# Moving the splits, the normalisation and the ranking of an attention and experts kernel into its batches of value matmuls

## The chip, the cores and the metric

One core of a Trainium2 chip (trn2) runs the whole program. The metric is the device time of one execution in microseconds (us). The median of 3 runs of the kernel before is 449.27 us (449.26 to 450.5).

## The reference

Four sequences of 256 tokens (D = 128) attend to a context of 1601 rows of 96 numbers, with 8 heads of 64, and then pass a mixture of 8 experts (2 chosen for each token) and one shared expert. Everything is float32.

```python
def xattn(x, context, Wq, Wk, Wv, Wo, bo):       # x is _layernorm(x)
    q = (x @ Wq).reshape(B, S, HEADS, DIM_HEAD).transpose(0, 2, 1, 3)
    k = (context @ Wk).reshape(B, L, HEADS, DIM_HEAD).transpose(0, 2, 1, 3)
    v = (context @ Wv).reshape(B, L, HEADS, DIM_HEAD).transpose(0, 2, 1, 3)
    attn = jax.nn.softmax(jnp.einsum('bhsd,bhld->bhsl', q, k) * scale, axis=-1)
    out = jnp.einsum('bhsl,bhld->bhsd', attn, v)
    return out.transpose(0, 2, 1, 3).reshape(B, S, INNER) @ Wo + bo
x = x + xattn(_layernorm(x), ctx_768, ...)
flat = _layernorm(x).reshape(T, d)
router_probs = softmax(flat @ router_w + router_b); topk_probs, topk_idx = top_k(router_probs, 2)
shared_out = gelu(flat @ sw1 + sb1) @ sw2 + sb2
h1 = gelu(einsum('td,edh->teh', flat, rw1) + rb1)
mixed = einsum('ted,te->td', einsum('teh,ehd->ted', h1, rw2) + rb2, weights)
x = x + shared_out + mixed
```

## The kernel before

The attention runs over 16 **pairs** of heads: 4 batches b times 4 pairs p, numbered 4b+p, so that pairs 0, 4, 8 and 12 open a batch. A pair has 13 chunks of 128 context rows (the last has 65), taken in 7 units of two chunks (the last unit has one). For each chunk TensorE (PE) computes the scores as three matmuls (lines 1165 to 1167), because each float32 operand is held as a high part in fp32r and a low part, the remainder; ScalarE (ACT) takes the exponential into `probs` (L766). When all scores of a pair are done, PE runs the pair's **batch of values**: 52 matmuls in the profile's count (L1181), probabilities times `v_sb`. After the batch come the **row sums** of the pair (L1046), a matmul with ones over the probabilities that were added up over the chunks. Adding them up is GpSimd's (POOL): one instruction for units 0 and 1 (L522) and one for each of units 2 to 5 (L524), each 128x1024; VectorE (DVE) then folds the two halves and adds unit 6 (L526, L527). PE's row sums wait for L527. In pair 0 POOL does L526 and L527 too, and in pairs 13 (units 4 and 5), 14 and 15 DVE does the adding.

Every engine goes through one list, `steps`, which `plan` writes: `main` is the order by hand (scores, quotients, and steps that follow an earlier pair by 2, 3 or 6 pairs, the table `behind`), and tasks for later pairs (maxima L1092 and L890, `g`) are put between by `plan`'s estimates. An engine takes from the list the steps that concern it, in order. These steps are touched by the change:

- **ctx**: the context of the next batch is split in 4 quarters, the high part by ACT (`high_part`, L705), the low part by POOL (`low_part`, L630). In batch b's pair p = 1 they stand one behind each of units 1 to 4, so between POOL's adds.
- **normalisation** of the tokens after attention: DVE takes moments in step `yt` (two pairs later, unit 3), POOL computes the inverse roots (L612 to L615, four small instructions) at the same step, and ACT writes the normalised tokens (`norm`, L711) behind unit 5, before the pair's last exponential.
- **rank** and **best**: the two largest router probabilities, on DVE (L938 to L952), then the weights on POOL (L669 to L674), behind unit 4 of pair 10.
- **w1**: the experts' first weights (128x2304) are split by POOL ahead of its loop (L651, L653). The raw weights lie at the start of `work`, whose first half is POOL's accumulators (two of 1024 columns, for pairs of even and odd number) and whose second half is `oT`, the attention's output (1024 columns for each of two batches), written by DVE in `quotient` (L837, L839).
- **stats**: the inverse roots of the first normalisation of batches 1 to 3, three times four small instructions on POOL in pair 0.

Of the kernel before, what the change touches and what calls it, by code (L numbers as in the profile page):

```python
# [52 lines left out]
def plan(batches, pairs, chunks, heads_per_pair, tiles, blocks, halves, experts):  # L53
# [3 lines left out]
    n_units = len(units)  # L57
    order = [(b, p) for b in range(batches) for p in range(pairs)]
    tasks = [("g", 0, 0)]
    n_v0 = 0  # L60
    for n, (b, p) in enumerate(order):
# [16 lines left out]
        if n == 0:  # L78
# [6 lines left out]
    behind = {(1, 2): [("ring", ("y",))], (3, 2): [("ring", ("yt",))], (5, 2): [("norm",)],  # L85
              (2, 3): [("ring", ("xt",))], (3, 3): [("ring", ("router",)), ("exp",)],
              (4, 3): [("rank",), ("best",)], (3, 6): [("ring", ("wrow",))]}
    main, held = [], []
    for n, (b, p) in enumerate(order):
        for u, unit in enumerate(units):  # L90
            for j, c in enumerate(unit):
                if p == 0 and b:
                    main.append(("ring", ("v", b, c)))
                main.append(("scores", (b, p, u, j)))
                if n and (u, j) in (((4, 0), (4, 1)) if n == 1 else ((0, 1), (1, 1))):
                    main.append(("quotient", order[n - 1] + ((u, j) in ((4, 1), (1, 1)),)))
            if (n, u) == (1, 3):
                main.append(("sums", order[0]))
            if p == 1 and b + 1 < batches and 0 < u <= blocks:
                main.append(("ctx", (b + 1, u - 1)))  # L100
            held += [("values", (b, p, u, j)) for j in range(len(unit))]
            if (b, p) == order[-2]:
                main += [("w2", e) for e in range(experts) if e * n_units // experts == u]
            for ago in (2, 3, 6):
                if n < ago:
                    continue
                qb, qp = order[n - ago]
                half = (qb + 1) * halves // batches - 1
                for x in behind.get((u, ago), []):
                    name = x[1][0] if x[0] == "ring" else x[0]  # L110
                    if qp == pairs - 1 and name in ("y", "yt", "xt"):
                        main.append(("ring", (name, qb)))
                    elif qp == pairs - 1 and name == "norm":
                        main.append((name, qb))
                    elif qp == pairs - 1 and (qb + 1) % (batches // halves) == 0:
                        main.append(("ring", (name, half)) if x[0] == "ring" else (name, half))
        main += held + [("sums", (b, p))] * (0 < n < len(order) - 1)
        held = []
# [6 lines left out]
    pe = dve = act = 0.0  # L125
# [30 lines left out]
    for i, x in enumerate(main):  # L156
        kind, w = x
# [47 lines left out]
def plan_experts(experts, chunks, halves, last_pair):  # L205
# [5 lines left out]
    b = last_pair[0]  # L211
# [6 lines left out]
    behind = {2: [("ring", ("yt", b))], 3: [("norm", b)]}  # L218
# [30 lines left out]
def build(nc, x, ctxT, WqkT, Wv, Wo, bo, router_w, router_b, sw1, sb1, sw2, sb2, rw1, rb1, rw2, rb2, out):  # L249
# [7 lines left out]
    T = S // P  # L257
# [15 lines left out]
    TH = HALF // P  # L273
    WLO = 32
# [29 lines left out]
    with ExitStack() as ctx:  # L304
# [3 lines left out]
        def sem(name):  # L308
            return ctx.enter_context(nc.semaphore(name))
# [47 lines left out]
        w1_sb = work[:].rearrange("p a b -> p (a b)")[:, 0:NE * H].rearrange("p (e h) -> p e h", e=NE)  # L357
# [79 lines left out]
        w_split = sem("w_split")  # L437
# [156 lines left out]
        def _(pool):  # L594
# [3 lines left out]
            def own(ins):  # L598
                done[0] += 1
                ins.then_inc(pool_done, 1)  # L600
# [48 lines left out]
            pool.wait_ge(s_w1, 32)  # L649
            pool.wait_ge(s_rw, 32)  # L650
            own(g.tensor_copy(w1_hi[:], w1_sb))  # L651
            then_own(g.tensor_copy(rw_hi[:], rw_sb[:]))
            g.tensor_tensor(w1_lo[:], w1_sb, w1_hi[:].bitcast(F32), ALU.subtract).then_inc(w_split, 1)  # L653
# [7 lines left out]
            pool.wait_ge(w_split, 3)  # L661
            pool.wait_ge(wrow_zero, 2)
            for kind, w in steps:
# [15 lines left out]
                if kind == "stats":  # L679
                    inverse_roots(slice(w * T, w * T + T), w + 1)  # L680
                if kind == "ring" and w[0] == "yt":
                    inverse_roots(slice(w[1] * T, w[1] * T + T), B + w[1] + 1)
# [14 lines left out]
        def _(act):  # L697
# [9 lines left out]
            def normal(src, tiles, round_no):  # L707

                act.wait_ge(rstd_ready, round_no)
                for t in tiles:  # L710
                    ins = nc.scalar.activation(xn[:, t, :], src[:, t, :], ACT.Identity, bias=shift[:, t:t + 1],  # L711
                                               scale=rstd[:, t:t + 1])
                ins.then_inc(xn_ready, 1)
# [11 lines left out]
            for kind, w in steps:  # L725
# [6 lines left out]
                elif kind == "normal":  # L732
                    normal(x_sb, range(w * T, w * T + T), w + 1)
                elif kind == "norm":
                    if w == 0:
                        act.wait_ge(*taken(("xn", 1)))
                    normal(x1, range(w * T, (w + 1) * T), B + w + 1)
# [70 lines left out]
        def _(dve):  # L808
# [189 lines left out]
        def _(pe):  # L998
# [51 lines left out]
            for kind, w in steps:  # L1050
                if kind == "sums":
                    row_sums(*w)
                if kind == "ring":
# [59 lines left out]
                    elif w[0] == "router":  # L1113
                        pe.wait_ge(w_split, 3)
# [83 lines left out]
                elif kind == "first":  # L1198

                    n, (h, e, k) = w, items[w]  # L1200
                    if n == 0:
                        pe.wait_ge(probs_ready, B * PAIRS * CH)
                        pe.wait_ge(w_split, 3)
# [60 lines left out]
```

## Time and profile before

| | |
|---|---|
| median of 3 runs | 449.27 us (449.26 to 450.5) |
| the profiled execution's own time | 449.95 us |
| its span, first to last instruction | 448.2 us |
| mean granted TensorE clock | 0.991 of full speed |
| PE busy | 432.9 us (97%) |
| DVE busy | 279.8 us (62%) |
| POOL busy | 257.9 us (58%) |
| ACT busy | 219.2 us (49%) |
| DMA packets | 7.30 MB, mean 16 GB/s |

The profile is of one execution. "Busy" is the time in which an engine has at least one instruction in work; a matmul's end is modelled, so a busy PE may be waiting for a fraction of a microsecond. The granted clock has two levels, 2.4 GHz (1.00) and 1.2 GHz (0.50). A bracket behind an instruction in the timeline tells how long its engine sat idle before it, and which instruction ended that.

### The profile page before, as it was taken

How to read it: one execution, taken by the hardware profiler on the slowest of the kernel's cores; microseconds unless marked ns; L12 is line 12 of the kernel's file. 1: busy time of each engine (PE TensorE's matmuls, PEld its weight loads, DVE VectorE, ACT ScalarE, POOL GpSimd, SP SyncE). 2: the span in 40 equal slices, each digit the busy share in tenths (PEclk: the TensorE clock that was granted, in tenths of full speed). 3: DMA queues.
4: the chain of work that ended last, by engine and by line, in shares of the span. 5: the costliest groups of instructions: out<-in, count | busy, mean ns of one | idle time of the engine just before them, and what ended most of it. 6: DMA issues, size and time to landing. Idle time of an engine off the chain costs nothing. (4 is left out here: it accounts for less than half of the span.)

```text
span 448.2 us, 7203 instructions
## 1 busy us (share of the span) xinstructions
PE 432.9 (97%) x2505; PEld 333.4 (74%) x2505; DVE 279.8 (62%) x555; ACT 219.2 (49%) x384; POOL 257.9 (58%) x183
## 2 busy tenths in 40 slices
PE   9999998999999979999999799999999999999996
PEld 7787767786877758777878586868776776777885
DVE  4785858695566648574458387844495775648443
ACT  3555524242752615335726152637334845686673
POOL 4979692746461938391719564635426620667771
PEclk9999999999999989999999999999999999999999
DMA  8300010000000020000000300000000000000000
GB/s 244 104 2 0 2 33 24 0 2 2 1 0 2 2 55 2 0 2 0 1 1 1 107 1 2 1 2 0 2 0 2 1 1 1 0 0 2 25 1 23
DMA packets 13834, 7.30 MB, mean 16 GB/s; under 512 B 9284, under 2 KB 12776, under 8 KB 13800
## 3 DMA queue, kind: packets, MB, share of 16 engines
q1 hardware_dynamic: 13800, 6.85, 6.2%
q8 instruction: 21, 0.34, 0.3%
q14 instruction: 13, 0.11, 0.1%
HBM read 6.29 MB, written 0.52 MB: 15 GB/s over the span
## 5 line engine op out<-in xcount | busy, mean ns | idle before, releaser
L766 ACT ACTIVATE probs<-ps 128x512 f32<-128x512 f32 (+1 forms) x208 | 123.8, 597 | 157.1 <-PE ps L1167 150.4
L890 DVE TENSOR_REDUCE maxes<-ps 128x1 f32<-128x402 f32 x256 | 131.7, 567 | 53.3 <-PE ps L1092 53.2
L524 POOL TENSOR_TENSOR work<-work,probs 128x1024 f32<-128x1024 f32 x54 | 128.8, 2385 | 14.3 <-ACT probs L766 12.3
L522 POOL TENSOR_TENSOR work<-probs 128x1024 f32<-128x1024 f32 x14 | 33.5, 2393 | 111.4 <-issue 107.7
L1181 PE MATMUL ps<-probs,v_sb 128*64 128x256 f32 (+1 forms) x832 | 93.4, 381 | 0.8 <-ACT probs L766 0.8
L1181 PEld LDWEIGHTS ps<-probs,v_sb 128*64 128x64 f32 (+1 forms) x832 | 59.1, 137 | 34.2 <-ACT probs L766 4.1
L1165 PE MATMUL ps<-g_hi,ctxT_hi 97*128 97x512 f32 (+1 forms) x208 | 84.4, 406 | 0.0
L1166 PE MATMUL ps<-g_lo,ctxT_hi 96*128 96x512 f32 (+1 forms) x208 | 82.8, 398 | 0.0
L1167 PE MATMUL ps<-g_hi,ctxT_lo 96*128 96x512 f32 (+1 forms) x208 | 82.3, 396 | 0.0
L1092 PE MATMUL ps<-ctxT_hi,g_hi 96*128 96x402 f32 x256 | 73.3, 363 | 0.4 <-DVE maxes L890 0.3
L690 POOL TENSOR_TENSOR g_lo<-probs,g_hi 128x512 fp32r<-128x512 f32 x32 | 40.6, 1292 | 35.5 <-ACT g_hi L788 34.3
L1092 PEld LDWEIGHTS ps<-ctxT_hi,g_hi 96*128 96x128 f32 x256 | 47.3, 191 | 14.8 <-issue 3.8
L1167 PEld LDWEIGHTS ps<-g_hi,ctxT_lo 96*128 96x128 f32 (+1 forms) x208 | 39.3, 189 | 10.2
L1165 PEld LDWEIGHTS ps<-g_hi,ctxT_hi 97*128 97x128 f32 (+1 forms) x208 | 38.9, 187 | 6.4 <-issue 0.8
L1166 PEld LDWEIGHTS ps<-g_lo,ctxT_hi 96*128 96x128 f32 (+1 forms) x208 | 39.3, 189 | 4.1
L526 DVE TENSOR_TENSOR work<-work 128x512 f32<-128x512 f32 x15 | 10.8, 719 | 38.3 <-POOL work L524 35.6
L837 DVE RECIPROCAL rden<-ps 128x128 f32<-128x128 f32 x32 | 30.3, 948 | 6.3 <-PE ps L1046 6.3
L744 ACT COPY v_sb<-ps 128x512 f32<-128x512 f32 (+1 forms) x39 | 22.9, 587 | 23.0 <-PE ps L1006 19.5
L976 DVE TENSOR_TENSOR probs<-ps,probs 128x512 f32<-128x512 f32 x32 | 20.6, 684 | 21.4 <-PE ps L1134 13.7
L803 ACT ACTIVATE probs<-ps,biasT 128x512 f32<-128x512 f32 x36 | 24.6, 688 | 17.7 <-PE ps L1006 16.0
L884 DVE CAST g_hi<-ps 96x512 fp32r<-96x512 f32 x16 | 10.9, 684 | 19.0 <-PE ps L1006 19.0
L1004 PE MATMUL ps<-wv_hi,ctxT_hi 96*128 96x512 f32 (+1 forms) x52 | 21.1, 406 | 0.1
(149 smaller groups left out, 536.1 us busy)
## 6 DMA issues: line engine op xcount, KB each, us to landing
raw<-in_ctx_T_dram SPq DMA_DIRECT2D x3, 600.4 KB, 4.4
work<-in_L_ffn_rw_dram SPq DMA_DIRECT2D x1, 1024.0 KB, 7.1
g_hi<-neg_row SPq DMA_DIRECT2D x60, 0.5 KB, 2.0
raw<-in_ctx_T_dram SPq DMA_DIRECT2D x3, 150.8 KB, 2.6
x_sb<-in_x_dram SPq DMA_DIRECT2D x1, 384.0 KB, 5.3
early<-in_WqkT_dram SPq DMA_DIRECT2D x1, 336.0 KB, 4.5
wo_sb<-in_L_xattn_Wo_dram SPq DMA_DIRECT2D x1, 256.0 KB, 5.1
out_dram<-x_sb SPq DMA_DIRECT2D x1, 256.0 KB, 2.2
```

The source lines that it names most:

```text
L522: ops.tensor_tensor(acc, probs[:, (n - 1) % SLOTS], pr, ALU.add).then_inc(summed, 1)
L524: ops.tensor_tensor(acc, acc, pr, ALU.add).then_inc(summed, 1)
L690: g.tensor_tensor(hid_lo[:, w % SPLITS, :], activations(w), hid_hi[:, w % SPLITS, :].bitcast(F32), ALU.subtract).then_inc(hid_lo_ready, 1)
L766: nc.scalar.activation(probs[0:rows, n % SLOTS, j, :], s_bank(chunk_no(*w))[0:rows, :], ACT.Exp, scale=SCALE).then_inc(probs_ready, 1)
L803: nc.scalar.activation(hid[:, n % 4, :], ps[:, n % HB, :], ACT.Gelu, bias=biasT[:, c:c + 1]).then_inc(hid_ready, 1)
L837: v.reciprocal(rden[:, q], sums_bank[:, q]).then_inc(rden_ready, 1)
L890: v.tensor_reduce(maxes[:, p % 2, i * T + t, blk:blk + 1], src[:, 0:BW], AX.X, ALU.max).then_inc(ring_taken, 1)
L1092: ins = mm(dst[:, 0:BW], g_hi[0:C, b % 2, 2 * p + i, t * P:(t + 1) * P], ctxT_hi[0:C, b % 2, k0:k0 + BW], start=True, stop=True)
L1165: mm(dst, ctxT_hi[:, b % 2, ks], gh, start=True, stop=False)
L1166: mm(dst, ctxT_hi[0:C, b % 2, ks], gl, start=False, stop=False)
L1167: ins = mm(dst, ctxT_lo[:, b % 2, ks], gh[0:C], start=False, stop=True)
L1181: ins = mm(o_bank[DH * i:DH * (i + 1), :], v_sb[0:rows, c, h * DH:(h + 1) * DH], probs[0:rows, n % SLOTS, j, i * S:(i + 1) * S], start=(c ...
```

## The change

It moves steps in the list, and splits w1 in two. In short:

- The four ctx steps of the next batch stand together at the end of a pair's scores, just before its batch of values: in pair 1 for batch 1, and in pairs 4 and 8 (the first pair of a batch instead of the second) for batches 2 and 3.
- The inverse roots are a step of their own (`roots`) and stand with `norm` at the same place, in pairs 5, 9 and 13.
- rank and best stand behind the batch of values of pair 10.
- w1 is split in two parts, experts 0 to 4 (128x1280) at the end of pair 0 and the rest (128x1024) at the end of pair 2. The raw weights are loaded to the last 2304 columns of `work`, over the last 256 columns of the odd accumulator and over both halves of `oT`; so DVE waits in the quotients of pairs 0 and 4 for the part that lies there.
- The three `stats` roots become one call over six columns (`stats` 3).

```diff
-    behind = {(1, 2): [("ring", ("y",))], (3, 2): [("ring", ("yt",))], (5, 2): [("norm",)],
+    behind = {(1, 2): [("ring", ("y",))], (3, 2): [("ring", ("yt",))], (n_units, 2): [("roots",), ("norm",)],
               (2, 3): [("ring", ("xt",))], (3, 3): [("ring", ("router",)), ("exp",)],
-              (4, 3): [("rank",), ("best",)], (3, 6): [("ring", ("wrow",))]}
+              (n_units + 1, 3): [("rank",), ("best",)], (3, 6): [("ring", ("wrow",))]}
...
-            if p == 1 and b + 1 < batches and 0 < u <= blocks:
-                main.append(("ctx", (b + 1, u - 1)))
             held += [("values", (b, p, u, j)) for j in range(len(unit))]
...
+            main += followers(n, u)
+        if p == (b == 0) and b + 1 < batches:
+            main += [("ctx", (b + 1, k)) for k in range(blocks)]
+        main += [("w1", k) for k in range(2) if n == 2 * k] + followers(n, n_units)
+        held += followers(n, n_units + 1)
         main += held + [("sums", (b, p))] * (0 < n < len(order) - 1)
...
+    W1_CUT = NE - PAIRS
...
-        w1_sb = work[:].rearrange("p a b -> p (a b)")[:, 0:NE * H].rearrange("p (e h) -> p e h", e=NE)
+        w1_sb = work[:].rearrange("p a b -> p (a b)")[:, 4 * PAIRS * S - NE * H:].rearrange("p (e h) -> p e h", e=NE)
...
-            pool.wait_ge(s_w1, 32)
             pool.wait_ge(s_rw, 32)
-            own(g.tensor_copy(w1_hi[:], w1_sb))
             then_own(g.tensor_copy(rw_hi[:], rw_sb[:]))
-            g.tensor_tensor(w1_lo[:], w1_sb, w1_hi[:].bitcast(F32), ALU.subtract).then_inc(w_split, 1)
...
+                if kind == "w1":
+                    es = (slice(0, W1_CUT), slice(W1_CUT, NE))[w]
+                    pool.wait_ge(s_w1, 32)
+                    then_own(g.tensor_copy(w1_hi[:, es], w1_sb[:, es]))
+                    g.tensor_tensor(w1_lo[:, es], w1_sb[:, es], w1_hi[:, es].bitcast(F32), ALU.subtract
+                                    ).then_inc(w1_split, 1)
+                    pool.wait_ge(w1_split, w + 1)
+                if kind == "stats" and w == B - 1:
+                    inverse_roots(slice(T, NT), B)
+                if kind == "roots":
+                    inverse_roots(slice(w * T, w * T + T), B + w + 1)
...
+                if p == 0 and b < 2:
+                    dve.wait_ge(w1_split, b + 1)
                 v.tensor_tensor(oT[:, b % 2, p, q], o_bank[:, q], rden[:, q], ALU.mult).then_inc(sums_taken, 1)
```

How the instructions stand, first **POOL from the end of pair 0 to pair 2**. Before (L522 opens a pair's adds, L630 is a ctx low part):

```order
L526 TENSOR_TENSOR work<-work 128x512
L527 TENSOR_TENSOR work<-work,probs 65x512
L522 TENSOR_TENSOR work<-probs 128x1024
L630 TENSOR_TENSOR ctxT_lo<-raw,ctxT_hi 96x402
L524 TENSOR_TENSOR work<-work,probs 128x1024
```

and with the change (the lines have moved on by 9: L531 is the old L522, L533 the old L524, L639 the old L630; L688 and L689 split w1, whose name stands here without its number):

```order
L535 TENSOR_TENSOR work<-work 128x512
L536 TENSOR_TENSOR work<-work,probs 65x512
L688 CAST w_hi<-work 128x1280
L689 TENSOR_TENSOR w_lo<-work,w_hi 128x1280
L531 TENSOR_TENSOR work<-probs 128x1024
L533 TENSOR_TENSOR work<-work,probs 128x1024 x4
L639 TENSOR_TENSOR ctxT_lo<-raw,ctxT_hi 96x402 x3
L639 TENSOR_TENSOR ctxT_lo<-raw,ctxT_hi 96x395
L531 TENSOR_TENSOR work<-probs 128x1024
L533 TENSOR_TENSOR work<-work,probs 128x1024 x4
L688 CAST w_hi<-work 128x1024
L689 TENSOR_TENSOR w_lo<-work,w_hi 128x1024
```

The low parts no longer stand between pair 1's adds but behind all five, and the two parts of w1 stand behind pair 0 and pair 2.

**POOL in pair 5**, before:

```order
L522 TENSOR_TENSOR work<-probs 128x1024
L630 TENSOR_TENSOR ctxT_lo<-raw,ctxT_hi 96x402
L524 TENSOR_TENSOR work<-work,probs 128x1024
L612 TENSOR_SCALAR veps<-mv 128x2
L613 TENSOR_TENSOR rstd<-veps,neg_half 128x2
L614 TENSOR_TENSOR shift<-mv,rstd 128x2
L615 TENSOR_SCALAR shift<-shift 128x2
L630 TENSOR_TENSOR ctxT_lo<-raw,ctxT_hi 96x395
```

and with the change:

```order
L531 TENSOR_TENSOR work<-probs 128x1024
L533 TENSOR_TENSOR work<-work,probs 128x1024 x4
L621 TENSOR_SCALAR veps<-mv 128x2
L622 TENSOR_TENSOR rstd<-veps,neg_half 128x2
L623 TENSOR_TENSOR shift<-mv,rstd 128x2
L624 TENSOR_SCALAR shift<-shift 128x2
```

Pair 5's four low parts have gone to the end of pair 4, and its roots stand behind the fifth add. Pair 9 reads the same. On PE nothing moves but three maxima of pair 10, which stand ahead of its batch of values instead of behind it.

## Rows read from the trace of the kernel before

**Rows 1.** Waits of PE: instruction waiting <- releaser: us in total, times, longest.

```profile
PE ps L1046 <- DVE work L527: 8.4, 5, 3.1
```

**Rows 2.** Timeline of PE: start, us, instruction [idle before]; pairs 1, 2, 4.

```profile
61.21 5.83 PE L1181 MATMUL ps<-probs,v_sb 128*64 128x256 f32 x52 [0.77 <-ACT probs L766]
...
68.60 0.65 PE L1046 MATMUL ps<-work,ones 128*64 128x256 f32 x4 [1.55 <-DVE work L527]
...
83.49 5.83 PE L1181 MATMUL ps<-probs,v_sb 128*64 128x256 f32 x52
89.15 0.60 PE L1046 MATMUL ps<-work,ones 128*64 128x256 f32 x4
...
137.62 0.60 PE L1046 MATMUL ps<-work,ones 128*64 128x256 f32 x4
```

**Rows 3.** Timeline of PE; pairs 5, 9 and 10.

```profile
153.45 5.84 PE L1181 MATMUL ps<-probs,v_sb 128*64 128x256 f32 x52
162.37 0.65 PE L1046 MATMUL ps<-work,ones 128*64 128x256 f32 x4 [3.08 <-DVE work L527]
...
254.50 0.65 PE L1046 MATMUL ps<-work,ones 128*64 128x256 f32 x4 [2.52 <-DVE work L527]
...
278.14 0.65 PE L1046 MATMUL ps<-work,ones 128*64 128x256 f32 x4 [0.81 <-DVE work L527]
```

**Rows 4.** Stretches: us, busy us (instructions) by engine, granted clock, DMA share, GB/s.

```profile
66.00:70.00 4.00, 2.45 (x21) 1.52 (x18) 1.38 (x2) 0.00 (x0) 1.10 (x1) 1.00 0.48 141
163.00:167.00 4.00, 4.00 (x14) 3.52 (x13) 3.08 (x7) 0.60 (x1) 0.00 (x0) 0.57 0.00 0
255.00:259.00 4.00, 4.00 (x13) 3.44 (x12) 2.96 (x6) 0.60 (x1) 0.00 (x0) 0.57 0.36 120
```

**Rows 5.** Timeline of POOL; pairs 0 to 2, then 4 and 5.

```profile
46.96 1.29 POOL L527 TENSOR_TENSOR work<-work,probs 65x512 f32<-65x512 f32 x1
51.95 2.40 POOL L522 TENSOR_TENSOR work<-probs 128x1024 f32<-128x1024 f32 x1 [3.71 <-ACT probs L766]
...
77.58 9.78 POOL L524 TENSOR_TENSOR work<-work,probs 128x1024 f32<-128x1024 f32 x4
...
130.49 2.38 POOL L524 TENSOR_TENSOR work<-work,probs 128x1024 f32<-128x1024 f32 x1 [0.74 <-ACT probs L766]
143.44 2.38 POOL L522 TENSOR_TENSOR work<-probs 128x1024 f32<-128x1024 f32 x1 [10.57 <-issue]
145.78 1.05 POOL L630 TENSOR_TENSOR ctxT_lo<-raw,ctxT_hi 96x402 fp32r<-96x402 f32 x1
...
153.66 0.22 POOL L612 TENSOR_SCALAR veps<-mv 128x2 f32<-128x2 f32 x1
...
155.22 2.36 POOL L524 TENSOR_TENSOR work<-work,probs 128x1024 f32<-128x1024 f32 x1
```

**Rows 6.** Timeline of DVE: quotient of pair 0, last add of pair 2.

```profile
57.16 0.95 DVE L837 RECIPROCAL rden<-ps 128x128 f32<-128x128 f32 x1
...
88.12 0.69 DVE L527 TENSOR_TENSOR work<-work,probs 65x512 f32<-65x512 f32 x1
```

**Rows 7.** Groups of POOL: the w1 split, xcount | busy, mean ns of one.

```profile
L653 POOL TENSOR_TENSOR w_lo<-work,w_hi 128x2304 fp32r<-128x2304 f32 x1 | 5.2, 5153 | 0.1
...
L651 POOL CAST w_hi<-work 128x2304 fp32r<-128x2304 f32 x1 | 2.1, 2109 | 0.0
```

**Rows 8.** Timeline: DVE adds at 340 and 355.72, POOL's veps at 340.28.

```profile
340.23 1.23 DVE L524 TENSOR_TENSOR work<-work,probs 128x1024 f32<-128x1024 f32 x1 [1.66 <-POOL work L524]
340.28 1.26 POOL L612 TENSOR_SCALAR veps<-mv 128x2 f32<-128x2 f32 x1
...
355.72 5.01 DVE L524 TENSOR_TENSOR work<-work,probs 128x1024 f32<-128x1024 f32 x3
```

**Rows 9.** Groups of POOL: six low parts of w2, then three beside DVE's adds.

```profile
L677 POOL TENSOR_TENSOR ctxT_hi<-raw,w_hi 128x256 fp32r<-128x256 f32 x6 | 5.4, 924 | 7.0 <-ACT w_hi L750 6.8
...
L677 POOL TENSOR_TENSOR ctxT_lo<-raw,w_hi 128x256 fp32r<-128x256 f32 x3 | 5.1, 1711 | 0.0
```

More of the change, by code:

```diff
@@ L83, in plan, with followers @@
     last_max = {t[1:3]: n + 1 for n, t in enumerate(tasks) if t[0] == "max"}
-    behind = {(1, 2): [("ring", ("y",))], (3, 2): [("ring", ("yt",))], (5, 2): [("norm",)],
+    behind = {(1, 2): [("ring", ("y",))], (3, 2): [("ring", ("yt",))], (n_units, 2): [("roots",), ("norm",)],
               (2, 3): [("ring", ("xt",))], (3, 3): [("ring", ("router",)), ("exp",)],
-              (4, 3): [("rank",), ("best",)], (3, 6): [("ring", ("wrow",))]}
+              (n_units + 1, 3): [("rank",), ("best",)], (3, 6): [("ring", ("wrow",))]}
+    def followers(n, u):
+        found = []
+        for ago in (2, 3, 6):
+            if n < ago:
+                continue
+            qb, qp = order[n - ago]
+            half = (qb + 1) * halves // batches - 1
+            for x in behind.get((u, ago), []):
+                name = x[1][0] if x[0] == "ring" else x[0]
+                if qp == pairs - 1 and name in ("y", "yt", "xt"):
+                    found.append(("ring", (name, qb)))
+                elif qp == pairs - 1 and name in ("roots", "norm"):
+                    found.append((name, qb))
+                elif qp == pairs - 1 and (qb + 1) % (batches // halves) == 0:
+                    found.append(("ring", (name, half)) if x[0] == "ring" else (name, half))
+        return found
     main, held = [], []
@@ L103, in plan @@
                 main += [("w2", e) for e in range(experts) if e * n_units // experts == u]
[L104 to L116, printed above, removed]
+            main += followers(n, u)
[3 more added lines that the diff above has]
+        held += followers(n, n_units + 1)
         main += held + [("sums", (b, p))] * (0 < n < len(order) - 1)
@@ L217, in plan_experts @@
             5: [("ring", ("router", last)), ("exp", last)], 6: [("rank", last), ("best", last)], 8: [("ring", ("wrow", last))]}
-    behind = {2: [("ring", ("yt", b))], 3: [("norm", b)]}
+    behind = {2: [("ring", ("yt", b)), ("roots", b)], 3: [("norm", b)]}
     out, n, waiting, weighted = [], 0, [], []
@@ L436, in build @@
         consts_ready = sem("consts_ready")
-        w_split = sem("w_split")
+        w_split, w1_split = sem("w_split"), sem("w1_split")
         rstd_ready = sem("rstd_ready")
@@ L658, in _ @@
             g.memset(wrow[:, :, E:E + 1], 1.0).then_inc(wrow_zero, 1)
-            pool.wait_ge(w_split, 3)
+            pool.wait_ge(w_split, 2)
             pool.wait_ge(wrow_zero, 2)
@@ L678, in _ @@
                                     ).then_inc(w2_split, 1)
[L679 to L682, printed above, removed]
+                if kind == "w1":
[9 more added lines that the diff above has]
+                    inverse_roots(slice(w * T, w * T + T), B + w + 1)
                 if kind == "split":
@@ L732, in _ @@
                 elif kind == "normal":
-                    normal(x_sb, range(w * T, w * T + T), w + 1)
+                    normal(x_sb, range(w * T, w * T + T), 2)
                 elif kind == "norm":
@@ L736, in _ @@
                         act.wait_ge(*taken(("xn", 1)))
-                    normal(x1, range(w * T, (w + 1) * T), B + w + 1)
+                    normal(x1, range(w * T, (w + 1) * T), w + 3)
                 elif kind == "ring" and w[0] == "v":
@@ L1113, in _ @@
                     elif w[0] == "router":
-                        pe.wait_ge(w_split, 3)
+                        pe.wait_ge(w_split, 2)
                         pe.wait_ge(*taken(("xt", (b + 1) * B // NHALF - 1)))
@@ L1202, in _ @@
                         pe.wait_ge(probs_ready, B * PAIRS * CH)
-                        pe.wait_ge(w_split, 3)
+                        pe.wait_ge(w1_split, 2)
                     if n >= HB:
```

## Prediction

> **What bounds the kernel now.** I read the page first: TensorE (PE) is busy 97% of the span, so only PE's idle time and its clock can give anything. Second, the waits of PE: one entry holds nearly all of it, the row sums (L1046) waiting for VectorE's (DVE's) last add L527, 8.4 us in five waits [rows 1]. Third, the timeline at those places [rows 2, 3]: the waits are 1.55 us in pair 1, 3.08 in pair 5, 2.52 in pair 9, 0.81 in pair 10, and 0.4, what is left of the total, in pair 13. The true loss is a little larger. In pair 2, where nothing is waited for, the batch of values starts at 83.49 and the row sums at 89.15, 5.66 us later, though the batch is drawn as 5.83 us long [rows 2]. Each of the five waits hides some 0.18 us more, 0.9 in all, so 9.3 us. Fourth, the granted clock in stretches: after pair 5's wait and after pair 9's it is 0.57 over 4 us, that is 1.2 GHz for most of it, and 4 x (1 - 0.57) = 1.7 us of full clock are gone each time; after pair 1's wait of 1.55 us it stays at 1.00 [rows 4]. Two of those make 3.4 us. What could be had is 9.3 + 3.4 = 12.7 us.
>
> Why is L527 late? GpSimd (POOL) needs 12.2 us for its five adds of a pair (2.38 + 9.78) [rows 5] and has just time for them. In pairs 1, 5 and 9 it also does four low parts of 1.05 us between them, and in pairs 5 and 9 the inverse roots, from 153.66 to the next add at 155.22, 1.56 us [rows 5]. Between pairs it idles: 10.57 us before pair 5's first add [rows 5]. In pair 10 the fifth add stands behind `best`, and `best` behind DVE's ranking; in pair 13 ScalarE's (ACT's) last exponential stands behind `norm`, which waits for the roots.
>
> **The change, part by part.** The sum is made against the profiled execution (449.95 us, span 448.2), which lies 0.7 us above the median of the runs, 449.27; I take the differences from the median.
>
> *Pairs 5 and 9.* In pair 5 POOL's adds start at 143.44 and run through: 143.44 + 12.2 = 155.6. DVE's two adds of 0.69 us follow [rows 6], so 157.1, and with the roots now queued behind the fifth add and meddling (below) at most 1.6 us more. PE comes to the row sums at 153.45 + 5.66 = 159.1 [rows 3]. The wait goes, and the low clock behind it: 3.08 + 0.18 + 1.7 = 5.0 us. Pair 9 is built the same: 2.52 + 0.18 + 1.7 = 4.4 us. `norm` on ACT then waits for the roots, until about 158.5; queued behind it are the next pair's exponentials, whose first scores PE can't have before about 161. Nothing.
>
> *Pairs 10 and 13.* The fifth add of pair 10 no longer waits for the ranking: 0.81 + 0.18 = 1.0 us. Ranking on DVE now runs while PE finishes the batch, and the three maxima that moved ahead of the batch cost PE what they cost behind it. In pair 13 the last exponential no longer waits for `norm`: 0.4 + 0.18 = 0.6 us.
>
> *Pairs 4 and 8* take over four low parts on POOL and four casts on ACT, behind the last add and the last exponential. Pair 4's last add ends at 130.49 + 2.38 = 132.9 [rows 5], PE's row sums start at 137.62 [rows 2]: 4.7 us for DVE's 1.4, so even two low parts in between are hidden. The low parts, 4.2 us, lie in the 10.57 us gap. Nothing.
>
> *Start and pair 0.* POOL's two passes over w1 (2.11 and 5.15 us) [rows 7] leave the start, where PE did not wait for them: nothing won. By columns, the first part costs 2.11 x 1280/2304 + 5.15 x 1280/2304 = 4.0 us. POOL is done with pair 0 at 46.96 + 1.29 = 48.25, perhaps 0.6 earlier without two rounds of roots, so w1's part ends between 51.8 and 52.3. Pair 1's first add started at 51.95, when its exponentials were there [rows 5]. It costs 0 to 0.3 us, taken as 0.
>
> *Pair 1.* Adds from 51.95 to 64.1, PE at the row sums at 61.21 + 5.66 = 66.9 [rows 2]: a margin of 2.8 us for DVE's 1.4. I leave the 0.77 us ahead of the batch alone: a quotient on DVE ends just there, and DVE's order is unchanged. Behind the fifth add stand four low parts, which brings in the one cost that this change adds.
>
> *POOL beside DVE's last adds.* L526 and L527 read two tensors of SBUF, and every POOL instruction moved here reads SBUF too. The rows show what happens when such instructions meet: POOL's `veps`, 0.22 us alone [rows 5], took 1.26 us when it began 0.05 us behind a DVE add of 1.23 us [rows 8]. It sat until the add was over. And where both engines keep coming they take turns: three DVE adds took 5.01 us, 1.67 each instead of 1.23 [rows 8], and POOL's low parts 1.71 instead of 0.92 [rows 9]. A turn of both takes 1.7 us, where 1.23 + 0.92 would be 2.15; so a handover overlaps by some 0.2 us. In pair 1: 1.05 (low part) + 0.69 (L526) + 1.05 + 0.69 (L527), less three handovers of 0.2, is 2.9 us against a margin of 2.8: 0.1 us stays. Of pair 1's 1.73 us, 1.6 goes.
>
> *Pair 2* is where it hurts. The fifth add ends at 77.58 + 9.78 = 87.36 [rows 5], L527 at 88.81 [rows 6], PE takes the row sums at 89.15: a margin of 1.8 us from the fifth add, of which 1.4 is used. Now w1's second part, by columns 0.94 us of cast and 2.29 us of subtraction [rows 7], is queued right behind that add. POOL needs no semaphore's way, so the cast starts first; L526 waits for it, the subtraction waits for L526, and L527, which needs L526's result, comes behind the subtraction: 0.94 + 0.69 + 2.29 + 0.69 = 4.6, less 0.6 for handovers, 4.0 us. PE waits 4.0 - 1.8 = 2.2, with hand-over time some 2.4 us. The bounds are 0 (the subtraction comes behind L527) and 4.6 - 1.8 = 2.8. The nearest waits are 2.52 us, which was followed by the low clock, and 1.55 us, which was not [rows 2 to 4]; 2.4 is next to the first, so I add 1.7 us. Pair 2 costs 4.1 us.
>
> The Trainium skill ("SBUF — State Buffer", section "Who interferes with whom") says that a DVE instruction with two SBUF inputs contends with a GpSimd instruction that reads SBUF, and that the second to issue fully blocks until the first is through. Taken to the letter it leaves no overlap at a handover, and the whole would come to 0.6 us more in pair 2 and 0.6 more in pair 1: 442.1 instead of 440.9. The rows agree with the blocking and not with the last 0.2 us of it.
>
> *Sum*: 5.0 + 4.4 + 1.0 + 0.6 + 1.6 - 4.1 = 8.5 us, with rounding in the terms 8.4. 449.3 - 8.4 = **440.9 us**.
>
> **Rivals.**
>
> 1. *No wait in pair 2.* POOL's cast reads one tensor and may not hold DVE up; then L526 runs at once, L527 at 0.72 us, before the subtraction is ready at 0.94, and nothing is lost: 440.9 - 4.1 = 436.8 us. For it: no row has a POOL cast beside a two-input DVE add. Against it: `veps` reads one tensor as well and was held up [rows 8]. If DVE gets in first and the cast second, L527 ends some 2.1 us behind the fifth add, 0.3 us of wait, 437.1 us. Together 0.23.
>
> 2. *The wait in pair 2 comes, the low clock does not*, since 2.4 lies between 1.55 and 2.52: 440.9 - 1.7 = 439.2 us. 0.12.
>
> 3. *More such waits.* If w1's first part ends at 52.3 and handovers give nothing, pair 1 is left with 0.35 + 0.7 = 1.0 us, and pair 2 with 0.4 more: 442.3 us; if pair 1's clock falls as well, 444. 0.10.
>
> 4. *Slower*: DVE's new wait in the quotient of pair 0. Everything behind it on DVE, the maxima and the second quotient, then waits for w1's first part, and PE's batch of pair 1, which already starts just as that quotient ends, waits too, one for one. DVE comes there at 57.16 [rows 6], POOL should be done at 52.3. It would have to be done after 57.16 + 8.4 = 65.6 for the kernel to lose, so the two passes would have to take 17 us where the columns give 4.0; from there on each microsecond is one lost, and at 20 us it would be 452 us. Nothing in the profile speaks for it. 0.03.
>
> 5. *Nothing happens*: the adds end as late as before because something other than the steps between them holds POOL. Pair 2 speaks against it: the same five adds, nothing between them, no wait. 449.3 us, 0.02.
>
> **How the numbers follow.** The forecast has 0.50, rivals 1 to 5 have 0.23, 0.12, 0.10, 0.02 and 0.03 (slower). A measurement of this kernel can tell about 0.3% (1.3 us) from no change. Faster by more than that: 0.50 + 0.23 + 0.12 + 0.10 = 0.95; within it 0.02; slower 0.03. The range reaches down to rival 1 with 0.5 us for the bounds, 436.3, and up to 443.6, in rival 3, which leaves out its upper end and the last two.
>
> **What would show it.** In the profile after: PE's waits for L527's successor in pairs 5, 9, 10 and 13 gone, and the clock at 1.00 behind pairs 5 and 9; one new wait of some 2.4 us before pair 2's row sums, near 89 us, with the clock at 0.5 behind it; DVE's two adds in pair 2 drawn as about 1.4 and 2.6 us long instead of 0.69, or the second begun late; POOL's low parts in pair 1 stretched. The prediction is wrong if pair 2's row sums start 5.66 us behind their batch (436.8 then), if pair 1 keeps more than 0.5 us, or if PE finds a new wait where the exponentials stand behind `norm` or the context casts.

## The result, and the profile after

The changed kernel took 442.96 us (median of 4 runs, 442.25 to 443.53), the kernel before 449.26 us. The ratio is 0.985, 95% interval 0.9833 to 0.9866: faster by 1.5%. The forecast was 440.9 us, its range 436.3 to 443.6. The profiled execution after has its own time of 443.53 us and a span of 441.7 us, 6.5 us less than before.

| | before | after |
|---|---|---|
| span | 448.2 us | 441.7 us |
| mean granted TensorE clock | 0.991 | 0.992 |
| PE busy | 432.9 us (97%) | 431.9 us (98%) |
| POOL busy | 257.9 us | 262.0 us |
| DVE busy | 279.8 us | 284.7 us |

POOL does the same work and is busy 4.1 us longer, DVE 4.9 us longer: the first sign that they get in each other's way. The clock's mean is hardly better, though two low stretches should have gone. The waits of PE, the answer to [rows 1] (L1061 is the old L1046, L536 the old L527):

```profile
PE ps L1061 <- DVE work L536: 3.0, 2, 2.3
```

Five waits of 8.4 us have become two of 3.0. The timeline of PE shows which, start in us, instruction, and in the bracket the idle time before it. Each pair of rows is a pair's batch of values and its row sums, here for pairs 1, 3 and 5, and for pair 2 the row sums alone; they answer to [rows 2, 3]:

```profile
61.02 5.83 PE L1196 MATMUL ps<-probs,v_sb 128*64 128x256 f32 x52 [0.77 <-ACT probs L779]
67.53 0.65 PE L1061 MATMUL ps<-work,ones 128*64 128x256 f32 x4 [0.68 <-DVE work L536]
...
90.58 0.65 PE L1061 MATMUL ps<-work,ones 128*64 128x256 f32 x4 [2.33 <-DVE work L536]
108.10 5.83 PE L1196 MATMUL ps<-probs,v_sb 128*64 128x256 f32 x52
113.76 0.65 PE L1061 MATMUL ps<-work,ones 128*64 128x256 f32 x4
...
157.82 5.83 PE L1196 MATMUL ps<-probs,v_sb 128*64 128x256 f32 x52
163.48 0.60 PE L1061 MATMUL ps<-work,ones 128*64 128x256 f32 x4
```

Pair 5's wait is gone. Pair 1 keeps 0.68 us, and pair 2, which waited for nothing before, has the new wait of 2.33 us. Stretches of the profile (us, busy us and instructions of PE, PEld, DVE, ACT, POOL, then the granted clock) answer to [rows 4]:

```profile
91.00:99.00 8.00, 8.00 (x27) 6.85 (x24) 6.38 (x14) 1.79 (x3) 0.00 (x0) 0.57 0.05 2
163.00:167.00 4.00, 4.00 (x25) 3.06 (x21) 2.50 (x6) 1.67 (x4) 0.44 (x2) 1.00 0.33 93
251.00:259.00 8.00, 8.00 (x46) 6.54 (x43) 6.52 (x13) 4.46 (x8) 2.50 (x3) 1.00 0.38 136
```

Behind pairs 5 and 9 the clock stays at full speed. Behind pair 2's new wait it is low, and for twice as long as behind either wait in the profile of the kernel before: 8 x (1 - 0.57) = 3.4 us of full clock lost in one piece. What held L536 is in the timelines of POOL and DVE at the end of pair 2:

```profile
86.20 1.04 POOL L688 CAST w_hi<-work 128x1024 fp32r<-128x1024 f32 x1
87.32 2.67 POOL L689 TENSOR_TENSOR w_lo<-work,w_hi 128x1024 fp32r<-128x1024 f32 x1
```

```profile
86.29 1.49 DVE L535 TENSOR_TENSOR work<-work 128x512 f32<-128x512 f32 x1 [2.70 <-POOL work L533]
87.81 2.71 DVE L536 TENSOR_TENSOR work<-work,probs 65x512 f32<-65x512 f32 x1
```

The two adds that took 0.69 us each [rows 6] are drawn as 1.49 and 2.71 us, one stretched over POOL's cast of w1, the other over its subtraction. They end 4.26 us behind the fifth add (86.26), where PE's margin is 1.8.

From the starts of the row sums the 6.5 us can be told apart, interval by interval (before - after; negative is a loss):

| interval between row sums | before | after | difference |
|---|---|---|---|
| start to pair 1 | 68.60 | 67.53 | 1.07 |
| pair 1 to 2 | 20.55 | 23.05 | -2.50 |
| pair 2 to 3 | 20.29 | 23.18 | -2.89 |
| pair 4 to 5 | 24.75 | 21.49 | 3.26 |
| pair 5 to 6 | 21.26 | 19.66 | 1.60 |
| pair 7 to 9 | 51.45 | 48.77 | 2.68 |
| pair 9 to 11 | 43.10 | 40.47 | 2.63 |
| pair 12 to 13 | 22.03 | 21.38 | 0.65 |

They add up to 6.5 us; the intervals not shown differ by under 0.1 us. In the first row 0.2 us are scatter and not a gain: pair 0's batch of values starts at 39.18 us before, at 38.95 after, and at 39.23 when the changed kernel was profiled once more (e11 below). From there to pair 1's row sums it is 29.42 us before and 28.58 after, so pair 1 gave 0.84 us. So 11.9 us were won, and 5.4 of them given back in pairs 2 and 3.

### The profile page after: what moved, and what is told of

Its sections match the earlier page's. It is cut to its first block, busy times and chain, and to the rows that moved or that the text cites. A ratio compares the mean times of both kernels' runs of the same rounds, so it can differ in the third digit from the quotient of the medians.

```text
span 441.7 us, 7201 instructions
## 1 busy us (share of the span) xinstructions
PE 431.9 (98%) x2505; PEld 333.5 (76%) x2505; DVE 284.7 (64%) x555; ACT 220.1 (50%) x384; POOL 262.0 (59%) x177
## 4 chain that ended last, share of the span: by engine, by line
PE 79%; POOL 11%; DVE 5%; issue 3%; ACT 1%; POOLq 0%; DVEq 0%; ACTq 0%
PE ps L1196 17%; PE ps L1180 9%; PE ps L1181 9%; PE ps L1107 9%; PE ps L1182 9%; PE ps L1019 7%; POOL work L533 6%; PE ps L1021 6%; PE ps L1020 6%; PE ps L1118 2%; PE ps L1061 1%; PE ps L1027 1%; DVE maxes L905 1%; POOL work L531 1%; POOL g_lo L703 1%
## 5 line engine op out<-in xcount | busy, mean ns | idle before, releaser
L533 POOL TENSOR_TENSOR work<-work,probs 128x1024 f32<-128x1024 f32 x54 | 128.7, 2384 | 17.1 <-ACT probs L779 14.3
L531 POOL TENSOR_TENSOR work<-probs 128x1024 f32<-128x1024 f32 x14 | 33.5, 2391 | 99.7 <-issue 77.8
L535 DVE TENSOR_TENSOR work<-work 128x512 f32<-128x512 f32 x15 | 13.4, 895 | 25.7 <-POOL work L533 25.6
```

The source lines that it names most:

```text
L531: ops.tensor_tensor(acc, probs[:, (n - 1) % SLOTS], pr, ALU.add).then_inc(summed, 1)
L533: ops.tensor_tensor(acc, acc, pr, ALU.add).then_inc(summed, 1)
```

## The experiments

The theory was the forecast's: POOL's second part of w1 holds DVE's last two adds of pair 2 back, by taking turns with them for SBUF, and the long wait on PE brings the low clock. Every kernel was timed beside the kernel before on the same chip; the two kernels of the result, e1 to e4, e5 to e8 and e9 to e12 are four such groups, and the kernel before took 449.26, 450.27, 449.88 and 450.21 us in them. So medians of different groups are compared through their ratios to it. The expectations start from 449.3 us or from the changed kernel's 443.0, so a miss of up to 1 us can come from that alone.

### What w1 costs in pair 2

**e1_w1_after_fold**: the changed kernel, POOL waits for DVE's last add of pair 2.

```diff
                     pool.wait_ge(s_w1, 32)
+                    if w:
+                        pool.wait_ge(summed, 3 * (NU - 1))
                     then_own(g.tensor_copy(w1_hi[:, es], w1_sb[:, es]))
```

> The changed kernel, but POOL waits for DVE's last add of pair 2 before it casts the second part of w1. Port theory: L527's successor in pair 2 ends 1.4 us behind the fifth add again, the wait of 2.33 us (2.5 with what the drawn end hides) before pair 2's row sums is gone, and so is the low clock from 91.4 to 98.0 us, which made pair 3 2.9 us longer: 442.3 to 443.0 less 5.4, 437.2 to 437.9 us. Rival (the clock falls there for a reason of its own): the wait goes, pair 3 stays 2.9 us longer, 440.4 us. Rival (the adds themselves are late): nothing changes, 443.0 us.

Measured: 438.27 us, ratio 0.9736 (0.9721 to 0.975). DVE and PE at the end of pair 2:

```profile
86.25 0.69 DVE L535 TENSOR_TENSOR work<-work 128x512 f32<-128x512 f32 x1 [2.72 <-POOL work L533]
86.98 0.69 DVE L536 TENSOR_TENSOR work<-work,probs 65x512 f32<-65x512 f32 x1
...
87.98 0.60 PE L1063 MATMUL ps<-work,ones 128*64 128x256 f32 x4
```

and the stretch behind it:

```profile
91.00:99.00 8.00, 8.00 (x40) 6.59 (x39) 7.86 (x17) 4.33 (x8) 4.77 (x3) 1.00 0.05 2
```

Both adds are back to 0.69 us, the bracket on the row sums is gone, and the clock is 1.00 in the stretch where it was 0.57. The median is 4.7 us below the changed kernel's and 0.4 to 1.1 us above what was expected; by the ratios it is 1.1%, 5.1 us, and the profiled execution's span is 5.5 us shorter (436.2 against 441.7). The two rivals (a clock that falls by itself, adds that are late by themselves) are out.

**e2_cast_first**: the same wait, but between the cast and the subtraction.

```diff
                     then_own(g.tensor_copy(w1_hi[:, es], w1_sb[:, es]))
+                    if w:
+                        pool.wait_ge(summed, 3 * (NU - 1))
                     g.tensor_tensor(w1_lo[:, es], w1_sb[:, es], w1_hi[:, es].bitcast(F32), ALU.subtract
```

> The changed kernel, but only the subtraction of w1's second part waits for DVE's last add of pair 2; the cast stays right behind the fifth add. If a cast with one input holds DVE up like a subtraction does: DVE's first add takes 1.5 us as it does now, the second 0.69, L536 ends 2.3 us behind the fifth add against a margin of 1.8, PE waits 0.3 to 0.5 us, and that is too short for the clock to fall: about 438.0 us. If it is the subtraction alone that counts: no wait, as e1_w1_after_fold.

Measured: 438.43 us, ratio 0.9742 (0.9727 to 0.9756).

```profile
86.66 1.49 DVE L535 TENSOR_TENSOR work<-work 128x512 f32<-128x512 f32 x1 [2.70 <-POOL work L533]
88.19 0.69 DVE L536 TENSOR_TENSOR work<-work,probs 65x512 f32<-65x512 f32 x1
...
88.93 0.65 PE L1063 MATMUL ps<-work,ones 128*64 128x256 f32 x4 [0.35 <-DVE work L536]
```

A cast, which reads one tensor, holds a DVE add up as the theory had it: 0.69 becomes 1.49 us beside a cast of 1.04. That is 0.35 us on PE, and the clock stays up, so nearly all of the loss is the subtraction's. The times of e1 and e2 can't be told apart; the rows can.

**e7_sub_half** and **e8_sub_three** let 2 and 3 of the 4 experts' subtraction run ahead of the wait, which makes PE's wait as long as one wants:

```diff
+                    if w:
+                        part, es = slice(es.start, es.start + 2), slice(es.start + 2, es.stop)
+                        g.tensor_tensor(w1_lo[:, part], w1_sb[:, part], w1_hi[:, part].bitcast(F32), ALU.subtract
+                                        ).then_inc(pool_done, 1)
+                        done[0] += 1
+                        pool.wait_ge(summed, 3 * (NU - 1))
                     g.tensor_tensor(w1_lo[:, es], w1_sb[:, es], w1_hi[:, es].bitcast(F32), ALU.subtract
```

> The changed kernel, but of the subtraction of w1's second part 2 of 4 experts stand behind the cast and the others wait for DVE's last add. DVE: 1.49, then 0.69 + 1.15 = 1.8; it ends 3.4 us behind the fifth add, PE waits 1.3 to 1.5 us. The clock stayed up behind 1.55 us in pair 1 of the kernel before, and fell behind 2.33 and 2.52: it stays up here, 439 us. If it falls, 442 us.

> As e7_sub_half, with 3 of 4 experts ahead of the wait: PE waits 1.9 to 2.0 us in pair 2, between the longest wait that left the clock up (1.55) and the shortest that let it fall (2.33). 439.6 us if it stays up, 442.5 if it falls. It shows too how long the low clock lasts: 6.6 us as after 2.33 us in the changed kernel, or 3.4 as after 2.52 and 3.08 in the kernel before.

Measured: e7 439.93 us, ratio 0.9779 (0.9764 to 0.9794); e8 441.24 us (439.64 to 441.94), ratio 0.98 (0.9777 to 0.9824). The row sums of pair 2 in e7, and in e8 with the clock behind them in the profiled execution:

```profile
89.77 0.65 PE L1067 MATMUL ps<-work,ones 128*64 128x256 f32 x4 [1.29 <-DVE work L536]
```

```profile
89.52 0.65 PE L1067 MATMUL ps<-work,ones 128*64 128x256 f32 x4 [1.82 <-DVE work L536]
```

```profile
91.00:99.00 8.00, 8.00 (x40) 6.50 (x39) 7.90 (x18) 3.94 (x7) 2.87 (x2) 1.00 0.05 2
```

In the profiled execution of e7 the wait of 1.29 us costs its own length and no clock (mean 1.000). Of the three others two read 1.000 and 0.998, but one reads 0.996 and took 440.91 us, the longest of the four. With 1.82 us it is the usual case: of e8's four executions one took 439.64 us with a mean clock of 0.999, the profiled one, the others 440.74 to 441.94 us with 0.995 or 0.996. A mean of 0.996 is what one stretch with 1.7 us of lost clock gives (1.7 / 440 = 0.004). Where it lay in the executions that were not profiled is not shown; kernels without such a wait (e1 to e5, e9, e10, e12) never read below 0.998.

**e11_changed_again**: the changed kernel once more.

> The changed kernel unaltered, beside the other runs of this call, to see how far its time and its mean granted clock scatter. In its first four executions 442.25 us went with a clock of 0.995 and 442.7 to 443.5 us with 0.992. I expect the same two values: the low clock behind pair 2's wait lasts 6.6 us in most executions and about 4 in some. If the length is fixed, all executions show 0.992.

Measured: 442.4 us (441.62 to 443.25), ratio 0.9831 (0.9816 to 0.9846). Its four executions had clocks of 0.996, 0.992, 0.992 and 0.995; the profiled one was the first:

```profile
91.00:99.00 8.00, 8.00 (x32) 6.67 (x33) 6.46 (x14) 2.69 (x5) 0.17 (x1) 0.79 0.05 2
```

Here the same wait (2.4 us) is followed by 8 x (1 - 0.79) = 1.7 us of lost clock instead of 3.4. Going by the mean clock, the low stretch was of the long kind in five of the changed kernel's eight executions (0.992) and of the short kind in three (0.995, 0.996). Time does not follow it alone: 442.31 us with 0.996 and 442.5 with 0.992. The kernel before scatters too: timed beside e1 to e12 it read 0.991 or 0.992 in 14 executions, as two short stretches give, and 0.987 or 0.988 in 9, so there was another short stretch or a long one in place of a short one. None of those nine was profiled.

### What is left in pair 1, and w1 as a whole

**e3_all_after_fold**: e1, and the context's low parts wait for DVE's last add of their pair.

```diff
                 if kind == "ctx":
+                    if w[1] == 0:
+                        pool.wait_ge(summed, ((w[0] - 1) * PAIRS + (w[0] == 1) + 1) * (NU - 1))
                     low_part(*w)
```

> e1_w1_after_fold, and the context's low parts in pairs 1, 4 and 8 wait for DVE's last add of their pair too. Pair 1's adds end at 64.8, DVE's two at 66.2, PE comes at 66.7: the wait of 0.68 us (0.86) goes, pairs 4 and 8 had room and change nothing. 0.9 us below e1_w1_after_fold, 436.3 to 437.0 us. If pair 1's wait comes from w1's first part, which made pair 1's adds 0.65 us late, and not from the port, 0.2 us or less is won.

**e4_w1_at_start**: the changed kernel, w1 split whole ahead of POOL's loop, as before the change.

```diff
+            pool.wait_ge(s_w1, 32)
             pool.wait_ge(s_rw, 32)
+            own(g.tensor_copy(w1_hi[:], w1_sb))
             then_own(g.tensor_copy(rw_hi[:], rw_sb[:]))
+            g.tensor_tensor(w1_lo[:], w1_sb, w1_hi[:].bitcast(F32), ALU.subtract).then_inc(w1_split, 2)
...
-        main += [("w1", k) for k in range(2) if n == 2 * k] + followers(n, n_units)
+        main += followers(n, n_units)
```

> The changed kernel, but w1 is split whole at the start, ahead of POOL's loop, where POOL idled 11.7 us in the changed kernel; all other moves stay. Pair 1's adds start at 51.95 instead of 52.59, so its wait falls from 0.86 to about 0.2; pair 2 has no wait and no low clock. 443.0 - 5.4 - 0.65 = 436.9 us. It tells what w1's move alone costs: 6 us by my reading, 0 by the reading that pair 2's wait comes from elsewhere.

**e10_start_and_fold**: both.

> w1 split at the start as in e4_w1_at_start, and the context's low parts behind DVE's last add as in e3_all_after_fold. In both of those no wait for DVE's last add is left, so there is nothing for the two together to win: 436.9 us, within 0.3 of either. Below 436.5 would mean that a wait is still hidden.

| | us | ratio to before (95%) |
|---|---|---|
| e3_all_after_fold | 436.86 | 0.9704 (0.969 to 0.9719) |
| e4_w1_at_start | 436.94 | 0.9709 (0.9692 to 0.9725) |
| e10_start_and_fold | 436.55 | 0.9705 (0.9692 to 0.9719) |

All three came as expected (e10 0.35 us below its number, but its ratio is e3's). In e3, DVE's adds of pair 1 and PE's row sums:

```profile
64.68 0.69 DVE L535 TENSOR_TENSOR work<-work 128x512 f32<-128x512 f32 x1 [2.97 <-POOL work L533]
65.41 0.69 DVE L536 TENSOR_TENSOR work<-work,probs 65x512 f32<-65x512 f32 x1
...
66.53 0.63 PE L1065 MATMUL ps<-work,ones 128*64 128x256 f32 x4
```

In e4 the adds are still stretched by the low parts, but pair 1's adds come early enough:

```profile
63.47 1.37 DVE L535 TENSOR_TENSOR work<-work 128x512 f32<-128x512 f32 x1 [2.13 <-POOL work L533]
64.87 1.27 DVE L536 TENSOR_TENSOR work<-work,probs 65x512 f32<-65x512 f32 x1
...
66.19 0.65 PE L1065 MATMUL ps<-work,ones 128*64 128x256 f32 x4
```

So pair 1's 0.68 us need both causes: the low parts beside DVE's adds, 1.3 us, and w1's first part, which made POOL late. Taking away either is enough. (e5 below, which leaves w1 alone and has the low parts behind pair 1's fifth add, shows no wait there either.) And the move of w1 costs 0.985 - 0.9709, 1.4% or 6.3 us, which is as much as the whole change gained.

### Which move gives the gain

**e5_only_ctx**: the kernel before, with the context steps alone moved (first diff). **e6_only_norm**: the kernel before, with roots and normalisation alone moved (second).

```diff
-            if p == 1 and b + 1 < batches and 0 < u <= blocks:
-                main.append(("ctx", (b + 1, u - 1)))
...
+        if p == (b == 0) and b + 1 < batches:
+            main += [("ctx", (b + 1, k)) for k in range(blocks)]
         main += held + [("sums", (b, p))] * (0 < n < len(order) - 1)
```

```diff
-    behind = {(1, 2): [("ring", ("y",))], (3, 2): [("ring", ("yt",))], (5, 2): [("norm",)],
+    behind = {(1, 2): [("ring", ("y",))], (3, 2): [("ring", ("yt",))], (6, 2): [("roots",), ("norm",)],
...
-                if kind == "ring" and w[0] == "yt":
-                    inverse_roots(slice(w[1] * T, w[1] * T + T), B + w[1] + 1)
+                if kind == "roots":
+                    inverse_roots(slice(w * T, w * T + T), B + w + 1)
```

> The kernel before, with the context steps alone moved to the end of a pair's scores. Pairs 5 and 9 lose 4.2 us of low parts between their adds and keep the 1.56 us of roots: adds end at 157.2, DVE at 158.6, PE comes at 159.1, so no wait and no low clock there: 5.0 + 4.4. Pair 1 keeps about 0.3 of 1.73. Pairs 10 and 13 stay. 449.3 - 5.0 - 4.4 - 1.4 = 438.5 us. Rival (each move gives its share): about a half of the gain, 444 us.

> The kernel before, with roots and normalisation alone moved to the end of a pair's scores. Pairs 5 and 9 lose 1.56 us between their adds, their waits fall from 3.08 and 2.52 to about 1.5 and 1.0; the clock stayed up behind 1.55 us in pair 1, so it should here, 1.7 us more each. Pair 13 gives 0.6. 449.3 - 2 x (1.56 + 1.7) - 0.6 = 442.2 us. If the clock falls all the same: 445.6 us.

Measured: e5 439.77 us, ratio 0.9771 (0.9757 to 0.9786); e6 443.23 us, ratio 0.9848 (0.9832 to 0.9865). The row sums of pairs 5, 9, 10 and 13 in e5:

```profile
157.79 0.65 PE L1046 MATMUL ps<-work,ones 128*64 128x256 f32 x4 [0.32 <-DVE work L527]
...
246.17 0.65 PE L1046 MATMUL ps<-work,ones 128*64 128x256 f32 x4 [0.33 <-DVE work L527]
...
268.25 0.65 PE L1046 MATMUL ps<-work,ones 128*64 128x256 f32 x4 [0.81 <-DVE work L527]
...
336.97 0.65 PE L1046 MATMUL ps<-work,ones 128*64 128x256 f32 x4 [0.44 <-DVE work L527]
```

I had expected pairs 5 and 9 free; each keeps 0.3 us (0.5 with what the drawn end hides), 1.0 us together. Pair 1 gave 0.3 us more than expected, and the kernel before took 449.88 us beside e5 instead of 449.3; the three make up the 1.3 us by which e5 missed. In e6 they keep more, here pair 5 (pair 1 keeps 1.51 us, pairs 9 and 10 0.80 each):

```profile
160.86 0.65 PE L1046 MATMUL ps<-work,ones 128*64 128x256 f32 x4 [1.43 <-DVE work L527]
```

```profile
160.00:170.00 10.00, 9.14 (x47) 7.61 (x48) 8.71 (x18) 5.16 (x10) 5.29 (x6) 1.00 0.05 12
```

and in this execution the clock stays at 1.00 behind 1.43 us. Its mean is 0.999 in two of e6's four executions and 0.996 and 0.995 in the others (443.3 and 443.39 us), so in those it seems to have fallen behind one of the waits of 1.4 to 1.5 us; they were not profiled. The rival of "each move its share" is wrong: moving 1.56 us of roots alone brings 1.5%, as much as the whole change, and moving the context alone 2.3%. They do not add up to 3.8%: e4, which has all moves but w1's, gains 2.9%. Either one alone makes the waits of pairs 5 and 9 so short that the profile shows no low clock behind them, and those 3.4 us (0.8%) are won once only.

### A version that beats both

PE still waits 0.77 us ahead of pair 1's batch. The profile names ACT's exponential, but the second quotient of pair 0 on DVE ends there (60.58 + 0.29 = 60.87 in the changed kernel, the batch starts at 61.02). **e9_fold_and_quotient** and **e12_start_fold_quotient** are e3 and e10 with the row sums and quotients of pair 0 one unit earlier:

```diff
-                if n and (u, j) in (((4, 0), (4, 1)) if n == 1 else ((0, 1), (1, 1))):
-                    main.append(("quotient", order[n - 1] + ((u, j) in ((4, 1), (1, 1)),)))
-            if (n, u) == (1, 3):
+                if n and (u, j) in (((3, 0), (3, 1)) if n == 1 else ((0, 1), (1, 1))):
+                    main.append(("quotient", order[n - 1] + ((u, j) in ((3, 1), (1, 1)),)))
+            if (n, u) == (1, 2):
```

> e3_all_after_fold, and in pair 1 the row sums and the two quotients of pair 0 stand one unit earlier. If the 0.77 us that PE still waits ahead of pair 1's batch of values come from the second quotient (it ends at 60.75, where the batch begins at 60.90), the wait goes: 436.1 us. If they come from ACT's exponential, as the profile's line names it, nothing changes: 436.9 us.

> e10_start_and_fold with the earlier quotients of e9_fold_and_quotient: 436.1 us if the quotient holds pair 1's batch, the same as e9_fold_and_quotient; 436.9 us if not.

Measured: e9 437.12 us, ratio 0.9711 (0.9698 to 0.9724), no gain over e3; e12 436.04 us (435.63 to 436.73), ratio 0.9688 (0.9675 to 0.9701). PE in e9, then in e12, at pair 1's batch and row sums:

```profile
60.32 5.83 PE L1200 MATMUL ps<-probs,v_sb 128*64 128x256 f32 x52
66.64 0.65 PE L1065 MATMUL ps<-work,ones 128*64 128x256 f32 x4 [0.49 <-DVE work L536]
```

```profile
60.40 5.83 PE L1202 MATMUL ps<-probs,v_sb 128*64 128x256 f32 x52
66.06 0.60 PE L1067 MATMUL ps<-work,ones 128*64 128x256 f32 x4
```

In both the 0.77 us are gone, so the quotient was the cause and not the exponential; in e9 the batch even starts at 60.32, before the pair's last exponential ends (60.65). In e9 the batch ends sooner than the adds, which w1's first part has made late, and 0.49 us come back as a wait for them; that is why e9 missed its 436.1 us. In e12, where w1 stands at the start, they don't, and it took what was expected. e12 is the fastest of all, 1.5% below the changed kernel timed beside it (e11, 0.9688 against 0.9831). Against e10 alone the intervals overlap, and the spans are 434.9 and 434.8 us; but pair 0's batch happened to start 1.0 us later in e12's profiled execution. From there to pair 2's row sums e12 takes 47.36 us and e10 48.14, 0.8 us less, while e9 and e3 take 48.14 and 48.17.

## Why the prediction was right, and where it was off

Its mechanism held where the time was won and lost: the waits of pairs 5, 9, 10 and 13 went, the new wait in pair 2 came, with the low clock behind it, and the time lay in the range. It was 2.1 us too low, and one of its own signs of being wrong came true: pair 1 kept 0.68 us (0.86 with what the drawn end hides), where it had said that more than 0.5 would refute it. By its own terms, from the table of intervals:

| term | forecast | measured |
|---|---|---|
| pair 5, wait and clock | 5.0 | 3.26 + 1.60 = 4.9 |
| pair 9 and pair 10, with clock | 4.4 + 1.0 | 2.68 + 2.63 = 5.3 |
| pair 13 | 0.6 | 0.65 |
| pair 1 | 1.6 | 0.84 |
| pair 2, wait | -2.4 | -2.50 |
| pair 2, low clock | -1.7 | -2.89 |

The measured terms add up to 6.3 us; the other 0.2 us by which the spans differ is the scatter at the start.

**Pairs 5, 9, 10, 13** came as worked out: the adds run through, POOL's roots behind them cost DVE nothing (the adds of pair 5 stay at 0.69 us each, since DVE took SBUF first), and `norm` held no exponential (in pair 5 it ends at 164.54, and the next exponential has its scores only at 165.74).

**Pair 2** was the one new cost and was there as described, cast first, subtraction in front of L527's successor: 4.26 us from the fifth add to the end of the adds, where the forecast had 4.0 and its bound 4.6; the interval grew by 2.5 us against 2.4. e1 and e2 show both halves of it. Rival 1, that a cast would not hold DVE up, is refuted by the 1.49 us of L535 in the changed kernel and in e2.

The Trainium skill's rule ("SBUF — State Buffer", "Who interferes with whom") is that the second to issue fully blocks until the first is through. Taken to the letter it gives 4.6 us for pair 2 by the forecast's prices, but these were too low: in e1, where nothing is beside them, the cast takes 1.04 us and the subtraction 2.39, not 0.94 and 2.29. With these it gives 1.04 + 0.69 + 2.39 + 0.69 = 4.8 us. Measured were 4.26, 0.55 less, so the trace agrees with the blocking and not with the full length of it, and the forecast's 0.2 us for each of three handovers was about right. In e2 the add ends 0.54 us behind the cast that it waited for (88.15 and 87.61), not 0.69, an overlap of 0.15 us.

**What failed** is the size of two terms. First "so I add 1.7 us" for the low clock, taken from the two stretches before; it measured 2.9 us, which is 1.2 of the 2.1 us missed. The same kernel shows a low stretch that costs 1.7 us in one execution and 3.4 in another, the longer one more often, and it was the longer in the profiled one, where 2.9 of the 3.4 us reached the row sums of pair 3. Rival 2, no low clock, did not occur in any of eight executions with the full wait, but it did in one of four at 1.82 us (e8). Second, "It costs 0 to 0.3 us, taken as 0" and with it "0.1 us stays" in pair 1, where 0.86 stayed. Two rounds of roots fewer did not bring POOL forward, because its roots then waited for DVE's last moments; w1's first part took 4.35 us (48.24 to 52.59) instead of 4.0, and pair 1's adds began 0.64 us late, in an execution in which PE was 0.2 us early:

```profile
48.24 1.25 POOL L688 CAST w_hi<-work 128x1280 fp32r<-128x1280 f32 x1
49.57 2.94 POOL L689 TENSOR_TENSOR w_lo<-work,w_hi 128x1280 fp32r<-128x1280 f32 x1
52.59 2.39 POOL L531 TENSOR_TENSOR work<-probs 128x1024 f32<-128x1024 f32 x1
```

The price by columns gives 1.17 and 2.86 us for these two instructions; measured are 1.25 and 2.94, and 0.08 us pass ahead of the subtraction and again ahead of the add. So PE's margin in pair 1 shrank from 2.8 us to 1.9 (the fifth add ends at 64.77, PE would come at 61.02 + 5.66 = 66.68), while the turns of low parts and adds took 2.7 us, even less than the forecast's 2.9.

Rival 3, with 442.3 us, lies nearest to the result, in part by luck. It had this late start, with 1.0 us kept in pair 1, but also 0.4 us more in pair 2, of which 0.1 came, and nothing of the longer low clock, which is the larger miss.

The remark that the 0.77 us ahead of pair 1's batch come from a quotient was right (e9, e12). Rivals 4 and 5 did not occur.

## What to carry to other kernels

Count whose turn it is at SBUF, not only who is idle: a POOL instruction put directly behind the one that DVE waits for runs beside DVE's next one, and if both read SBUF in the way these did, DVE pays for it. One semaphore wait, so that POOL starts behind DVE's short adds instead of ahead of them, turned a gain of 1.5% into 2.6% (e1), and a second one into 3.0% (e3).

A wait of TensorE can cost more than its own length. From 2.33 us on it brought a further 1.7 to 3.4 us of low clock in every execution here, and by the mean clock in some executions already at 1.3 to 1.8 us. Of two moves that each make such a wait short, the first brings that part of the gain and the second doesn't bring it again. Work out the margins in that light, and test moves one at a time: of what the other moves of this change gained, moving w1 gave back half.

## What was not expected of the hardware

- The low clock behind one and the same wait of PE has two lengths. Behind 2.33 us it cost 3.4 us (0.57 over 8 us), behind 2.4 us in another execution of the same kernel 1.7 us (0.79 over 8 us). In the profiled executions all waits up to 1.82 us left it up, but the mean clock says that this is no safe length: it reads 0.995 or 0.996 in one of four executions with a wait of 1.29 us (e7), in two of four with waits of 1.51 and 1.43 (e6) and in three of four with 1.82 (e8). With 2.33 us or more it was low in every execution. What decides whether it falls, and for how long, stays open.
- A short POOL instruction can lose as well as win. In pair 5 POOL's `veps` stands directly behind the fifth add, as the cast does in pair 2, but DVE got in first: its adds took 0.69 us each, and `veps` 0.73 instead of 0.22 us.

```profile
160.96 0.69 DVE L535 TENSOR_TENSOR work<-work 128x512 f32<-128x512 f32 x1 [2.35 <-POOL work L533]
...
161.01 0.73 POOL L621 TENSOR_SCALAR veps<-mv 128x2 f32<-128x2 f32 x1
```

The start in the timeline tells which: POOL's cast began 0.09 us before DVE's add (86.20 and 86.29), `veps` 0.05 us behind it. Why one instruction starts sooner behind an add than the other was not tried.
